# Moving the router's TensorE steps in a fused adaLN, attention and mixture-of-experts block

## What is computed

```python
def _L0_attn_ref(x, emb_weight, qkv_w, o_w):
    qkv = (x @ qkv_w.T).reshape(B, S, 3, N_HEAD, HEAD_DIM)
    q, k, v = (qkv[:, :, i].transpose(0, 2, 1, 3) for i in range(3))
    bias = emb_weight[_rel_buckets(S)].transpose(2, 0, 1)[None]
    scores = jnp.einsum('bhqd,bhkd->bhqk', q, k) * scale + bias
    attn = jax.nn.softmax(scores, axis=-1)
    a = jnp.einsum('bhqk,bhkd->bhqd', attn, v)
    return a.transpose(0, 2, 1, 3).reshape(B, S, N_HEAD * HEAD_DIM) @ o_w.T

def _L0_ffn_ref(hidden_states, router_w, expert_bias, w_gate, w_down, w_gate_shared, w_down_shared):
    logits = x @ router_w.T + expert_bias[None, :]
    probs = jax.nn.sigmoid(logits)
    top_w, top_idx = jax.lax.top_k(probs, 8)
    top_w = top_w / (jnp.sum(top_w, axis=-1, keepdims=True) + 1e-09) * 2.5
    combine = jnp.zeros((T, 160)).at[jnp.arange(T)[:, None], top_idx].set(top_w)
    h1 = jax.nn.silu(jnp.einsum('th,eih->eti', x, w_gate))
    routed = jnp.einsum('eti,ehi->th', h1 * combine.T[:, :, None], w_down)
    return routed + jax.nn.silu(x @ w_gate_shared.T) @ w_down_shared.T

h = _layernorm(x) * (1 + ca) + sa
x = x + ga * _L0_attn_ref(h, ...)
h = _layernorm(x) * (1 + cb) + sb
x = x + gb * _L0_ffn_ref(h, ...)
```

## Time and profile before

| what | value |
|---|---|
| runs | 1034.42, 1034.38, 1052.14 us (median 1034.42) |
| the profiled execution | 1034.07 us, with a span of 1031.3 us |
| PE matmul busy | 949.7 us (92%) |
| PE weight load (PEld) busy | 689.1 us (67%) |
| DVE busy | 781.3 us (76%) |
| ACT busy | 688.3 us (67%) |
| POOL busy | 402.4 us (39%) |
| granted PE clock, mean | 0.985 |

### The profile page before, as it was taken

One profiled execution on the slowest core, in us unless ns is written; L12 is line 12 of the kernel. 1 busy time (PEld: TensorE's weight loads), 2 busy tenths in 40 slices (PEclk: granted clock), 3 DMA queues, 4 the chain that ended last, 5 costly groups with the idle time before them and its releaser, 6 DMA issues. The chain is left out here.

```text
span 1031.3 us, 15705 instructions
## 1 busy us (share of the span) xinstructions
PE 949.7 (92%) x4596; PEld 689.1 (67%) x4596; DVE 781.3 (76%) x1487; ACT 688.3 (67%) x1161; POOL 402.4 (39%) x265
## 2 busy tenths in 40 slices
PE   4839999998899988999898779999999999999997
PEld 2526666655566555665554558888888888888886
DVE  5726766666666666666674479999999999999997
ACT  4626666675566755667563557777778787877785
POOL 0637888877688776887773000000000000000000
PEclk9969999999999999999999989999999999999999
DMA  7882554452534525345261089999999999999993
GB/s 211 263 209 62 124 125 101 102 123 62 144 85 113 123 63 142 83 115 123 62 163 54 17 212 220 218 214 218 215 217 215 218 217 218 216 217 217 216 217 91
DMA packets 72226, 160.58 MB, mean 156 GB/s; under 512 B 10496, under 2 KB 36416, under 8 KB 62448
## 3 DMA queue, kind: packets, MB, share of 16 engines
q1 hardware_dynamic: 72176, 159.97, 69.5%
HBM read 105.60 MB, written 2.42 MB: 105 GB/s over the span
## 5 line engine op out<-in xcount | busy, mean ns | idle before, releaser
L934 POOL TENSOR_SCALAR prob<-prob,rinv 128x512 f32<-128x512 f32 x256 | 398.1, 1568 | 147.4 <-DVE rinv L1079 145.4
L755 ACT ACTIVATE prob<-prob,nmax 128x512 f32<-128x512 f32 x256 | 182.9, 716 | 160.9 <-DVE nmax L1062 160.7
L632 PE MATMUL ps<-hT,wT 128*128 128x512 f32 x960 | 245.4, 392 | 1.9 <-DVE wT L1175 1.9
L1283 DVE TENSOR_TENSOR PT<-v_sb,strips 128x1024 f32<-128x1024 f32 x160 | 196.1, 1225 | 50.1 <-ACT v_sb L871 31.9
L871 ACT ACTIVATE v_sb<-ps 128x1024 f32<-128x1024 f32 x160 | 164.6, 1029 | 90.7 <-PE ps L632 89.6
L632 PEld LDWEIGHTS ps<-hT,wT 128*128 128x128 f32 x960 | 180.4, 189 | 42.6 <-DVE wT L1175 2.9
L632 PE MATMUL ps<-stack,wT 128*128 128x512 f32 x640 | 199.2, 393 | 9.1 <-DVE wT L1276 9.1
L1276 DVE TENSOR_TENSOR wT<-PT,stack 128x1024 fp32r<-128x1024 f32 x160 | 194.9, 1218 | 0.0
L208 DVE COPY PT<-ps 128x512 f32<-128x512 f32 x128 | 88.3, 690 | 127.1 <-PE ps L443 126.0
L1062 DVE CUSTOM_DVE_ANT_0 prob<-ps,strips 128x512 f32<-128x512 f32 x256 | 164.7, 680 | 13.7 <-PE ps L434 12.9
L862 ACT CAST stack<-PT 128x1024 fp32r<-128x1024 f32 x160 | 166.5, 1041 | 5.8 <-DVE PT L1283 5.8
(11 more groups left out here) (118 smaller groups left out, 691.7 us busy)
## 6 DMA issues: line engine op xcount, KB each, us to landing
strips<-comb_rows SPq DMA_DIRECT2D x152, 512.0 KB, 12.9
stack<-qk SPq DMA_DIRECT2D x128, 256.0 KB, 3.9
kLow<-qk SPq DMA_DIRECT2D x128, 128.0 KB, 3.8
strips<-bias_rows SPq DMA_DIRECT2D x3, 1792.0 KB, 15.1
strips<-in_L_ffn_w_gate SPq DMA_DIRECT2D x80, 64.0 KB, 12.4
strips<-in_L_ffn_w_down SPq DMA_DIRECT2D x80, 64.0 KB, 13.7
strips<-comb_rows SPq DMA_DIRECT2D x8, 256.0 KB, 5.2
strips<-comb_rows SPq DMA_DIRECT2D x16, 128.0 KB, 3.6
```

What stands on the lines that cost most here:

```text
L632: last = nc.tensor.matmul(ps[:, bank + c, :], weights(a), rows(m, c), start=start and k == 0, stop=stop and k == 2, skip_group_check=True)
L755: nc.scalar.activation(prob[:, u, :], prob[:, u, :], ACT.Exp, bias=nmax[:, u:u + 1], scale=-1.0, accum_out=rsum[:, u:u + 1]).then_inc(s_ex ...
L934: nc.gpsimd.tensor_scalar(prob[:, u, :], prob[:, u, :], rinv[:, u:u + 1], None, ALU.mult).then_inc(s_prob, 1)
L1283: nc.vector.tensor_tensor(weighted[:, k % 4, :], silu[:, k % 2, :], cb[:, r, half * HALF:(half + 1) * HALF], ALU.mult).then_inc(s_mul, 1)
```

## The change

It makes three edits. First, in `pair` on PE, the router steps of pairs 4 to 7 go from in front of the probability-value products of pair `n-2` to behind them (and behind `project_qk` of pair 0, where there is no router step). Second, the wait for `ld["small"]` leaves the place between pair 1 and pair 2 of batch 0, and stands ahead of the logits in pair 4 of every batch from 1 on. Third, for the last batch the router steps move forward in the stream of each of the three engines, and `first_down(3)` moves behind `shared_gate`.

```diff
--- before.py
+++ after.py
@@ -514,24 +514,21 @@
                 route = b - 1 if b >= 1 else None
                 scores(b, n, 0)
                 scores(b, n, 1)
-                if route is not None and n == 4:
-                    bank_free(b, n)
-                    logits(route, router_bank(n), 0)
-                    logits(route, router_bank(n + 1), 1)
-                if route is not None and n == 5:
-                    bank_free(b, n)
-                    transpose_sigmoids(route, router_bank(n), 0)
-                if route is not None and n == 6:
-                    bank_free(b, n)
-                    transpose_sigmoids(route, router_bank(n), 1)
-                if route is not None and n == 7:
-                    bank_free(b, n)
-                    transpose_comb(route, router_bank(n), 0)
                 if n >= 2:
                     attend(b, n - 2, 2)
                     attend(b, n - 2, 3)
                 if n == 0:
                     project_qk(b, 1)
+                if route is not None and n >= 4 and n <= 7:
+                    bank_free(b, n)
+                    if n == 4:
+                        pe.wait_ge(ld["small"], 80)
+                        logits(route, router_bank(n), 0)
+                        logits(route, router_bank(n + 1), 1)
+                    elif n == 7:
+                        transpose_comb(route, router_bank(n), 0)
+                    else:
+                        transpose_sigmoids(route, router_bank(n), n - 5)
                 if n >= 1:
                     transpose_probs(b, n - 1, 4)
                     transpose_probs(b, n - 1, 5)
@@ -590,7 +587,6 @@
             pair(0, 1)
             pe.wait_ge(w_split, 6)
             pe.wait_ge(ld["ow"], 16)
-            pe.wait_ge(ld["small"], 80)
             for b in range(B - 1):
                 for n in range(2, HPAIRS + 2):
                     pair(b, n)
@@ -676,22 +672,22 @@
             logits(late, ROUTER_B, 0)
             logits(late, ROUTER_A, 1)
             first_gate(2)
+            transpose_sigmoids(late, ROUTER_A, 0)
+            transpose_sigmoids(late, ROUTER_B, 1)
             first_gate(3)
             first_down(0)
-            transpose_sigmoids(late, ROUTER_A, 0)
-            transpose_sigmoids(late, ROUTER_B, 1)
             pe.wait_ge(s_h2l, B)
             first_gate(4)
+            pe.wait_ge(s_kept, 2 * B)
+            transpose_comb(late, ROUTER_A, 0)
+            transpose_comb(late, ROUTER_B, 1)
             first_down(1)
             first_gate(5)
             first_down(2)
-            first_down(3)
-            pe.wait_ge(s_kept, 2 * B)
-            transpose_comb(late, ROUTER_A, 0)
-            transpose_comb(late, ROUTER_B, 1)
             pe.wait_ge(s_cev, 2 * B)
             shared_gate(2)
             shared_gate(3)
+            first_down(3)
             shared_down(2)
             shared_down(3).then_inc(s_sd, 1)
             first_gate(6)
@@ -888,21 +884,21 @@
             shared_silu(0)
             shared_silu(1)
             gate_silu(0, 0)
+            sigmoids(late, (ROUTER_B, ROUTER_A))
+            h2_high(late)
             gate_silu(0, 1)
             product_high(0, 0)
-            h2_high(late)
-            sigmoids(late, (ROUTER_B, ROUTER_A))
             gate_silu(0, 2)
             product_high(0, 1)
             gate_silu(0, 3)
+            copy_comb(late, ROUTER_A, 0)
+            copy_comb(late, ROUTER_B, 1)
             product_high(0, 2)
             gate_silu(0, 4)
+            shared_silu(2)
+            shared_silu(3)
             product_high(0, 3)
             gate_silu(0, 5)
-            copy_comb(late, ROUTER_A, 0)
-            copy_comb(late, ROUTER_B, 1)
-            shared_silu(2)
-            shared_silu(3)
             product_high(0, 4)
             gate_silu(0, 6)
             product_high(0, 5)
@@ -1305,17 +1301,17 @@
                     dve.wait_ge(s_cb[r], 32)
                 weigh(0, k, r, half)
 
+            modulate2(late, ROUTER_A)
             first_weigh(0)
-            modulate2(late, ROUTER_A)
+            h2_low(late)
             first_weigh(1)
             product_low(0, 0)
-            h2_low(late)
+            keep_top(late, ROUTER_A, 0)
+            keep_top(late, ROUTER_B, 1)
             first_weigh(2)
             product_low(0, 1)
             first_weigh(3)
             product_low(0, 2)
-            keep_top(late, ROUTER_A, 0)
-            keep_top(late, ROUTER_B, 1)
             product_low(0, 3)
             first_weigh(4)
             first_weigh(5)
```

## The result

The changed kernel takes 1010.57 us (median of 4 runs, 1008.73 to 1011.11) against 1034.42 us for the kernel before, measured beside it. The latter is the median of three of its four runs; the fourth, 1052.14 us, was in a slower state, and medians and ratios here leave such runs out. The ratio is 0.9757, 95% interval 0.9731 to 0.9783. The forecast was 1009.3 us, 1003.0 to 1015.5. Its total is right to 1.3 us; one of its three terms is off by 3.2 us, and smaller differences the other way make up for a part of it. The profiled execution took 1011.11 us with a span of 1009.2 us, and a mean granted clock of 0.986.

What follows compares the result with a forecast made beforehand. PE's chain was taken as the bound, so any earlier start of round 1's matmul at 603.59 is gained in full: 1034.07 - 12.4 - 9.4 - 3.0 = 1009.3 us, with 8 in 10 from 1003 to 1015.5.

Steps and rivals of the forecast that it cites:

- Edit 2, -12.4 forecast: Batch 0, pair 2: without the small-loads wait PE starts at 62.42 instead of 74.84, 12.4 us earlier; range -14.3 to -10.5.
- The step that found the number: Before pair 2: ACT's cast at 62.42 waited for the same semaphore count, so the operands had landed; PE can start then.
- The charge for the clock: Pair 2 of batch 0: the clock is already low at 62.4, so the same 1.9 us cold start again, net nothing.
- the place of the sign steps: Pair 2 of batch 0: DVE's sign steps end at 66.2, then its first bias; PE needs that at 67.9.
- The rival of the sign steps: Pair 2 runs behind DVE's sign steps, counts from 64.8, and 2.4 us go: 1011.7 us; chance 0.08.
- its better end: Start of pair 2 of batch 0: no cold start, 1.9 us better, -14.3 instead of -12.4 us.
- Edit 1, -9.4 forecast: Attention pairs 4 to 7: PE's router waits go, 6.7 (pairs 5, 6), 2.1 (pair 7), 0.6 (pair 4); range 0 to -13.5.
- The rival made from the rule of the Trainium skill: Attention stage has slack and does not follow PE, so moving router steps pays nothing: 1018.7 us; chance 0.08.
- Edit 3, -3.0 forecast: Last batch: kept-weight copies end 8.0 us earlier, but round 1 starts only at 600.6 against 603.59; range -6 to 0.
- the new pauses drop it in the middle, 2 to 3 us go: Last batch: new PE pauses of 2.5 to 3 us lower the clock, costing 2 to 3 us.
- the rival that gives its gain back: Last batch: later silu, `product_high` behind the shared silu, clock falling twice; 0 to +2 us, 1012.3 to 1014.3; chance 0.16.
- The slow rival: Expert loop: routing rows, landing 12.9 us after issue, come late; a step lost per round, 49 us, 1058 us; chance 0.02.

Runs made afterwards that it cites:

- late pauses filled: Changed kernel plus matmuls nobody reads in three PE pauses of the last batch: 1005.87 us, ratio 0.9721.
- high part first with pauses filled: Changed kernel with product 3's high part ahead of the shared silus, and unread matmuls in three pauses (one before pair 2 of batch 0): 1001.45 us, ratio 0.9659.

## Why the prediction was right, and where not

**Edit 2, -12.4 forecast, -12.6 measured** at the start of pair 3, of which 0.5 us was already there at pair 1. The step that found the number, ACT's cast waiting for the same semaphore count, was right to 0.4 us. The charge for the clock (the same 1.9 us again) held too: pair 2 takes 2.2 us over 14.2. So did the place of the sign steps: I had DVE's bias start at 66.2 and PE need it at 67.9, and they came at 65.80 and 68.00. The rival of the sign steps, priced at 2.4 us, did not come at this clock. What the prediction did not see is that its better end, 1.9 us back with a full clock, was out of reach: at full clock the sign steps are next, and they keep 1.4 us of it.

**Edit 1, -9.4 forecast, -10.3 measured** from pair 3 to the last pair. Pair 4: forecast 0.2 us a pair, measured 0.25; the run with the logits in front confirms that ACT decides. Pairs 5 and 6: 1.13 us each, 1.46 in the one with the wait of 1.4, so all of the waits and a little more. Pair 7: 1.3 us each. Where the small surplus over the waits comes from was not tried. The rival made from the rule of the Trainium skill (Perfetto Trace Analysis, "Identifying the Most-Contended Engine"), to judge TensorE by the busy share of its weight loads (67% here) and not by that of its matmuls, gave 0 for this edit; this case's stages speak for the order of the instructions instead, 10.3 us.

**Edit 3, -3.0 forecast, +0.2 measured** at the start of round 1. This is the step that failed: the durations at full clock in a schedule whose pauses bring the clock down. The schedule up to the copies of the kept weights was right within 0.4 us (8.0 us earlier forecast, 8.4 measured); so was what is late next, `product_high` of step 3 behind the shared silu. I had worked the whole stretch with durations at full clock, and set "the new pauses drop it in the middle, 2 to 3 us go" only as the upper end. The clock fell behind two pauses of 2.5 and 2.9 us, and 3.2 us went: down product 3 started 1.2 us later than the schedule had it, and from there to round 1 it took 13.0 us instead of 11.0. With the pauses filled, round 1 starts 69.92 us behind the last pair, where the schedule has 600.6 - 530.7 = 69.9. But the 3.0 us were not a gain of the order alone. The schedule, at full clock, was set against a start of round 1 that was measured with half clock on the way; with that clock full as well, the old order takes 71.20 instead of 72.86 us. So of the 2.9 us, about 1.3 are the order's and 1.7 the clock's. For this edit the rival that gives its gain back (chance 0.16) came true, at the edge of its range of 0 to +2; its total, 1012.3 to 1014.3, did not.

That the sum came out right is in part luck. Against the forecast, the profile has 0.2 us more from edit 2, 0.9 more from edit 1 and 3.2 less from edit 3. From round 1 to the end of the span it takes 0.6 us more (the chain is 0.4 us shorter, the end behind the last matmul 1.0 us longer), and outside of the span 0.9 us less (1.9 instead of 2.8). That leaves the profiled execution 1.8 us above the forecast, and the median is 0.5 us below that execution. Only the first three have to do with the working. The slow rival, late rows in the expert loop, did not come: the chain is unbroken at 2.72 us a step. There is one place where DVE waits for rows, round 1 of the old order, in the kernel before already; the changed kernel does not wait there.

## What to carry to other kernels

A wait placed ahead of where its data is used costs the whole engine behind it, and is worth its length up to the next wait; look in the trace for another engine that waited for that next thing. A stop that goes is worth little where another engine holds the next rendezvous (pair 4: 0.25 of 1.57 us). In the last batch, where several engines hand work around, pauses of 2.4 to 3.6 us on TensorE cost twice, once as a pause and once as halved matmuls behind it; reorder so that the pause goes, or fill it, before judging an order by its time. And forecast both sides of a comparison at the same clock.

## What was not expected of the hardware

The granted clock fell behind pauses of 2.45 and 1.11 us with 1.06 us of transposes between them, and once, in the run with the later sign steps, behind 0.66 and 1.11 us, where the same pauses in two other runs (late pauses filled, and high part first with pauses filled) left it at 1.00. Useless matmuls in PE's pauses took 4.6 us off the time behind the last pair without one useful instruction moving in its order. And the median time from issue to landing of the loop's 512 KB row transfers was 12.9 us before, 6.4 us in the changed kernel, 6.6 us in its repeat, and between 6.3 and 13.1 us in the variants, while a step of the loop kept its 2.72 us in all fourteen profiles. What sets it was not tried. The slow rival rested on that one number; it says nothing of a bound while nobody waits for the rows.
